# Graph attention with routed feed-forward: GpSimd's order in a block, the projection in two halves, and where the feed-forward tiles begin

## What is computed

```python
x = x + _L0_gnn_ref(_layernorm(x, axis=-1), adj, ...)
x = x + _L0_ffn_ref(_layernorm(x, axis=-1), ...)

# in _L0_gnn_ref: 4 heads of 32, the keys in 8 chunks of 128, a softmax in every chunk
scores = jnp.einsum('bhnd,bhjcd->bhnjc', q, kc) / jnp.sqrt(jnp.asarray(Dh, dtype=q.dtype))
scores = jnp.clip(scores, -10.0, 10.0)
scores = jnp.where(mask == 0, jnp.asarray(-10.0, scores.dtype), scores)
attn = jax.nn.softmax(scores, axis=-1)
ctx = jnp.einsum('bhnjc,bhjcd->bhnd', attn, vc)
out = ctx @ Wo.T + bo
out = out + x        # then a layer norm with gamma and beta

# in _L0_ffn_ref: 8 experts of 128 -> 256 -> 128, the two best of each row
gate_scores = x @ Wg + bg
_, idx = jax.lax.top_k(gate_scores, K)
h = jax.nn.gelu(jnp.einsum('td,edh->teh', xf, W1) + b1[None], approximate=False)
y = jnp.einsum('teh,ehd->ted', h, W2) + b2[None]
out = jnp.einsum('ted,te->td', y, mf)
```

## Time and profile before

| what | before |
|---|---|
| median of 3 runs | 852.67 us (850.55 to 852.83) |
| the profiled execution | 852.1 us, of which the span from first to last instruction is 850.5 |
| granted TensorE clock, mean | 0.96 |
| PE busy | 722.9 us (85% of the span) |
| DVE busy | 626.5 us (74%) |
| ACT busy | 491.2 us (58%) |
| POOL busy | 591.9 us (70%) |
| first clamp of scores | at 38.3 us |
| last clamp of scores | at 592.1 us |
| first tile turned | at 609.2 us |

### The profile page before, as it was taken

One profiled execution on the slowest core, in us unless ns is written; L12 is line 12 of the kernel. 1 busy time (PEld: TensorE's weight loads), 2 busy tenths in 40 slices (PEclk: granted clock), 3 DMA queues, 4 the chain that ended last, 5 costly groups with the idle time before them and its releaser, 6 DMA issues. The chain is left out here.

```text
span 850.5 us, 17280 instructions
## 1 busy us (share of the span) xinstructions
PE 722.9 (85%) x5499; PEld 377.7 (44%) x5499; DVE 626.5 (74%) x1472; ACT 491.2 (58%) x873; POOL 591.9 (70%) x674
## 2 busy tenths in 40 slices
PE   2688998998989989899899898787577879999994
PEld 1222233232333333333323333231277768999994
DVE  2178898898988989889898898989774544455552
ACT  2456666766667666676665765635244535666662
POOL 4697665978779787797886977848764556445553
PEclk9989999999999999999999999998787989999998
DMA  7100000011010110101100001003211246432330
GB/s 260 62 1 25 14 13 13 13 39 50 14 39 13 39 50 13 39 13 39 50 13 26 14 27 37 14 26 110 76 54 57 68 133 189 123 85 85 102 93 1
DMA packets 45255, 45.43 MB, mean 53 GB/s; under 512 B 7413, under 2 KB 39424, under 8 KB 44720
## 3 DMA queue, kind: packets, MB, share of 16 engines
q1 hardware_dynamic: 38800, 30.00, 12.6%
q0 software_dynamic: 6368, 14.34, 4.8%
HBM read 31.46 MB, written 18.34 MB: 59 GB/s over the span
## 5 line engine op out<-in xcount | busy, mean ns | idle before, releaser
L641 ACT ACTIVATE e<-e 128x2048 f32<-128x2048 f32 x128 | 244.3, 1910 | 184.1 <-DVE e L783 181.3
L783 DVE SCALAR_TENSOR_TENSOR e<-scores_ps,bound_mem 128x2048 f32<-128x2048 f32 x128 | 291.9, 2281 | 43.8 <-PE scores_ps L393 42.4
L1189 POOL DMA_INDIRECT out<-e,near x91 | 90.3, 993 | 100.2 <-DVE e L964 51.7
L1167 POOL TENSOR_TENSOR ctx_part<-ctx_part,z_inv 128x1024 f32<-128x1024 f32 x62 | 119.8, 1933 | 49.1 <-DVE z_inv L799 49.1
L706 ACT ACTIVATE e<-scores_ps,bound_mem 128x128 f32<-128x128 f32 x364 | 103.8, 368 | 71.0 <-PE scores_ps L532 55.5
L412 PE MATMUL z_ps<-e,one_column 128*32 128x512 f32 x1024 | 137.4, 609 | 0.0
L1179 POOL TENSOR_TENSOR ctx_sum<-ctx_sum,ctx_part 128x512 f32<-128x512 f32 x90 | 115.8, 1287 | 6.0
L532 PE MATMUL scores_ps<-e,bound_mem 128*128 128x128 f32 x728 | 103.3, 287 | 13.7 <-DVE bound_mem L946 7.6
L532 PEld LDWEIGHTS scores_ps<-e,bound_mem 128*128 128x128 f32 x728 | 93.6, 201 | 17.4 <-issue 11.0
L946 DVE COPY bound_mem<-bound_mem 128x258 f32 x182 | 51.3, 324 | 55.6 <-issue 54.9
L791 DVE STREAM_TRANSPOSE ctx_part<-ctx_ps 128x512 f32<-128x512 f32 x128 | 90.1, 704 | 0.1
(11 more groups left out here) (156 smaller groups left out, 1046.7 us busy)
## 6 DMA issues: line engine op xcount, KB each, us to landing
near<-sorted_rows SPq DMA_DIRECT2D x91, 130.0 KB
near<-in_x SPq DMA_DIRECT2D x16, 256.0 KB
bound_mem<-in_adjT SPq DMA_DIRECT2D x4, 1024.0 KB, 11.0
x_post<-in_x SPq DMA_DIRECT2D x16, 256.0 KB, 2.7
sorted_rows<-sorted_rows SPq DMA_DIRECT2D x16, 130.0 KB
sorted_rows<-sorted_rows POOLq DMA_DIRECT2D x12, 130.0 KB
out<-e,near POOLq DMA_INDIRECT x91
sorted_rows<-x_rows,slot POOLq DMA_INDIRECT x64
```

The source lines that it names most:

```text
L641: nc.scalar.activation(every, every, ACT.Exp, scale=SCORE_SCALE).then_inc(exp_done, 1)
L783: dve.scalar_tensor_tensor(out=e[:, s % E_RING], in0=scores_ps[:], scalar=-CLIP, in1=to, op0=ALU.max, op1=ALU.min).then_inc(clipped, 1)
L1167: nc.gpsimd.tensor_tensor(pair, pair, z_inv[:, v % 2, j:j + 2].to_broadcast([P, 2, SQUARES, DH]), ALU.mult).then_inc(ctx_scaled, 1)
L1189: nc.gpsimd.indirect_dma_start(out=out_rows, out_offset=bass.IndirectOffsetOnAxis(ap=near_u[:, id_at:id_at + 1], axis=0), in_=e_flat[:, at ...
```

## The change

**Attention.** On POOL the adding and scaling of contexts stands ahead of each root: `add_context` 1 and `scale` 2 come before the root of `ln2`, and `add_context` 3 and `scale` 4 before the residual, and so on. In block 15 the scatter of block 12 moves from behind all that to right behind the first `scale`. PE projects two of four row groups at j = 1 and two at j = 2 (block 13 all at once, as before); the input is now turned back into the bank by a transpose, and the context product is summed onto it. `rank` moves from j = 5 to j = 6. `normalise_x` moves from j = 7 to j = 0 of the next block.

**Feed-forward.** Block 16 is gone. Slot 0 holds the first tile's turn, then the context of step 126 and the gates of block 13, slot 1 the second tile's turn, the context of step 127 and the projection of block 14. DVE copies the first tile's weights ahead of turning the last contexts, and reads each tile's offsets one slot ahead. Everything else that hung on slots is written two or three slots later. The pads are 12 on SP (two behind each load from tile 28 on), 10 on POOL and 6 on ACT (both from slot 22 on).

```diff
-SP_PADS = 16
-PAD_LOAD, PAD_SLOT = 19, 21
+SP_PADS, POOL_PADS = range(0, 12), range(12, 22)
+ACT_PADS = range(22, NP)
+PAD_LOAD, PAD_SLOT = 28, 22
...
-                if i >= PAD_LOAD and n_padded < SP_PADS:
-                    pad(n_padded)
-                    n_padded += 1
+                for k in SP_PADS[max(2 * (i - PAD_LOAD), 0):max(2 * (i - PAD_LOAD) + 2, 0)]:
+                    pad(k)
...
-            def project(v):
+            def project(v, tiles=range(TILES)):
...
-                for t in range(TILES):
+                for t in tiles:
                     cols = slice(t * P, (t + 1) * P)
-                    pe.matmul(job_ps[1][:, cols], ctxT[:, cols], w_proj[:, W_O, :], start=True, stop=False)
-                    ins = pe.matmul(job_ps[1][:, cols], xnT_bo[:, v % 4, cols], ident[:], start=False, stop=True)
-                ins.then_inc(proj_filled, 1)
+                    pe.transpose(job_ps[1][:, cols], xnT_bo[:, v % 4, cols], ident[:])
+                    ins = pe.matmul(job_ps[1][:, cols], ctxT[:, cols], w_proj[:, W_O, :], start=False, stop=True,
+                                    skip_group_check=True)
+                if TILES - 1 in tiles:
+                    ins.then_inc(proj_filled, 1)
...
-            for u in range(FIRST, BLOCKS + 1):
-                for j in range(CHUNKS if u < BLOCKS else LAG):
+            for u in range(FIRST, BLOCKS):
+                for j in range(CHUNKS):
...
-                    if j == (2 if last else 1) and is_block(u - 2):
-                        project(u - 2)
+                    if last and j == 2:
+                        project(13)
+                    if not last and j in (1, 2) and is_block(u - 2):
+                        project(u - 2, range(2 * j - 2, 2 * j))
...
-                    if j == (1 if last else 5) and is_block(u - 3):
+                    if j == (1 if last else 6) and is_block(u - 3):
                         rank(u - 3)
...
             for k in range(SLOTS):
...
-                if k == 5:
+                if k == 8:
                     project(15)
...
                 if k < FFN_TILES:
                     turn_tile(k)
+                if k < LAG:
+                    context(STEPS - LAG + k)
+                if k == 0:
+                    gate(13)
+                if k == 1:
+                    project(14)
...
+            def pad(k):
+                at = act.value_load(pad_at[0:1, k:k + 1], min_val=0, max_val=SPARE * P)
+                act.dma_start(sorted_rows[bass.ds(at, P), :], sorted_tiles[SPARE]).then_inc(padded_act, 16)
...
+                    if j == 0 and is_block(u + 2):
+                        normalise_x(u + 2)
...
-                    if j == 7 and is_block(u + 3):
-                        normalise_x(u + 3)
...
+            load_offsets(0)
             for k in range(SLOTS):
+                if k < FFN_TILES:
+                    copy_weights(k)
+                if k + 1 < FFN_TILES:
+                    load_offsets(k + 1)
+                if k < LAG:
+                    turn(STEPS - LAG + k)
                 if k == 0:
-                    scale_last(4)
-                    scale_last(6)
...
+                    choose(13)
+                if k == 1:
+                    invert_sums(15)
+                if k == 2:
                     dve.wait_ge(proj_filled, 15)
                     statistics(ln["2"], 14, job_ps[1][:].rearrange("p (t d) -> p t d", d=D))
...
             for u in range(FIRST, BLOCKS):
+                last = u == BLOCKS - 1
                 if is_block(u - 1):
                     scale(u - 1, 0)
+                if last:
+                    scatter(u - 3)
...
```

161 lines of the change are left out of this document (85 added, 76 removed).

## The result

The changed kernel takes **814.93 us** (median of 4 runs, 813.95 to 816.87) beside 852.75 us of the kernel before on the same chip (4 runs): a ratio of 0.956, 95% interval 0.9529 to 0.9591. The forecast was 816.5 us, in a range of 805 to 831, with the chance on faster. The profiled execution took 816.87 us, with a span of 815.2.

A forecast was written before the change was run, and what follows sets the result against it. It took attention as held by DVE's 32.0 us of waits for POOL's sum, the ramp by waiting, steady tiles by PE. Gains 21.2 + 2.4 + 2.6 + 4.2 + 2.6 + 5.6 - 3.0 = 35.6 us: 852.1 to 816.5, range 805 to 831.

The forecast's parts named there:

- The contexts' sum: Attention: POOL's sum comes in time for DVE's turn, 1.5 of 2.03 us a block gained, 21.2 us in all.
- Rival B: Attention: another wait, root and normalise of `ln3`, takes the place of the wait for POOL's sum; 832 us, chance 0.08.
- The rank: Attention: moving `rank` to j = 6 frees the scores of step 6, 0.2 us in 12 blocks, 2.4 us gained.
- The half clock: Attention, start of blocks after 5, 8 and 12's boundaries: half a projection and less idle time save 2.6 us.
- The projection in halves: Attention, j = 1 and 2: half projections with transposes fit where PE waits; taken as zero, -0.5 to +0.4 us a block.
- Rival C: Attention: transposes and short pauses bring PE's half clock everywhere; 875 us at three stretches a block, chance 0.03.
- The ramp: From attention's last blocks to the steady tiles: waits shrink, 9.4 us gained in all.
- The first slots: Ramp, slots 0 to 9: slot 10 comes 1.5 us after old slot 7 with three tiles more done, 4.2 us gained.
- The early scatter: End of attention: block 12's scatter fills POOL's idle time; SP's first tile load goes sooner, inserted waits of 1.3 us covered.
- The middle: Ramp, the next 17 slots: loads no longer late once pads wait behind load 28, 2.6 us gained.
- ACT's pads: Ramp, slots 22 to 27: six pads on ACT, taken at SP's 1.5 us each, partly hidden, 3 us lost.
- SP's pace: Ramp, last 11 slots: SP's loads and pads no longer set the pace, slots fall to 1.90 us, 5.6 us gained.

The follow-up runs named there:

- e1: Kernel before with only POOL's new order in the attention blocks: 815.78 us against 842.04 us, ratio 0.9684.
- e2: Changed kernel with POOL's order in the blocks put back as before: 833.01 us against 842.04 us for the kernel before, ratio 0.9888.
- r1: Kernel before with POOL's new order and `rank` at step 6, ramp left old: 824.75 us against 852.75 us, ratio 0.9671.
- before_again: Kernel before, unchanged, run and traced again on a chip like that of the first record: 852.76 us.
- e3: Changed kernel with the projection whole at step 1, as two products per tile: 813.09 us against 842.04 us for the kernel before, ratio 0.9647.
- e5: Changed kernel with `normalise_x` back at the end of step 7: 808.52 us against 842.04 us for the kernel before, ratio 0.9595.
- e9: Changed kernel with block 15's projection one slot later in PE's queue: 816.43 us against 852.75 us for the kernel before, ratio 0.9571.
- e6: Changed kernel with block 12's scatter back at the end of POOL's last block: 817.81 us against 842.31 us for the kernel before, ratio 0.9712.
- e7: Changed kernel with no pads on ACT, 14 on SP and 14 on POOL: 816.57 us against 842.31 us for the kernel before, ratio 0.9686.

## Why the prediction was right, and where its terms were off

**Attention, foreseen 26.2 us, measured 25.25.** Its parts, by the blocks' lengths:
- *The contexts' sum, 21.2 us.* Right in mechanism and size. e1 takes a block from 34.80 to 33.33, 1.47 us where 1.5 was foreseen, since PE's scores are next late, as the prediction read from its rows of PE; block 2 gains 1.72. Twelve blocks and that one are 19.4 us, where 21.2 was foreseen. Rival B (another wait in its place) did not come.
- *The rank, 2.4 us.* Measured 0.21 us a block, 2.5 in all. What the prediction did not see is that it hangs on the first term: alone, with POOL late, it gives nothing (e2).
- *The half clock, 2.6 us.* In the trace of before three blocks were 0.99 us longer than the rest, 3.0 us, and all of it went. The reason given, half a projection and less idle time, is right in its second half: contexts in time are enough, with the whole projection (r1), and the halves with late contexts leave the half clock where it was (e2). The blocks named were chance: in before_again it was 11 and 14, and not 5, 8 and 12. The row of slices, which the prediction names for them, can't show them; the stretches of the trace do.
- *The projection in halves, zero.* Right (e3). Step 0 became 0.05 us longer (4.80 to 4.85), but with the contexts in time and not with the halves: e1 and r1 have it, e2 does not. The working behind the zero misread its row: the projection was eight products of 0.22 us, 2 us in all, and not sixteen; a half takes 0.9 us here and not up to 1.2. Rival C, a half clock from transposes, is refuted by the clock: transposes stand in two steps of every block's projection, and from 48 us to the last clamp the granted clock was 1.00. The Trainium skill (TensorE: Matmul & The Clock Gate, Part 4: PE-mode transpose) gives a transpose of 128x128 some 275 ns in a kernel, for bf16, and says that they don't keep the clock up. Here, in float32, four in a row took 0.65 us, 0.16 us each, and the clock stayed up with products between them.

**The ramp, foreseen 9.4 us, measured 9.5** in the first pair of traces and 13.7 in the second, of which 3.8 come from POOL's order alone; its own edits give 8.4 us by times (r1). On the chips of 842 us they give some 3 (e1, e5). The sum is right on the chip that it was made for, and that is luck in part, since its terms were off in both ways:
- *The first slots, 4.2 us.* This term was mis-sized. Foreseen was tile 10 at 1.5 us behind the old tile 7. Measured from the last clamp it is 47.8 - 43.8 = 4.0 us in the first trace, so 1.7 were gained, and 44.6 - 43.8 = 0.8 in the second, 4.9 gained. The step that added up DVE's list slot by slot missed that PE is queued behind DVE's turn of block 15's contexts in the same slot, 4.4 to 5.1 us. It also charged to DVE what is a chain over four engines: e9 takes the wait at the projection away and gets it back at the root.
- *The early scatter* stands in no term of its own, and is the largest: e6 loses some 10 us without it. It was treated under the end of attention as covered by the experts' loads; SP's 12.3 us wait had in fact set the start of everything in the slots.
- *The middle, 2.6 us, and ACT's pads, -3.0.* Together -0.4 was foreseen and 65.8 - 62.5 = 3.3 measured. The pads cost nothing (e7), since a pad holds ACT's queue for 0.53 us: the error was to take SP's price, with SP's idle times in it, for another engine. With them on ACT the last pad is in time for tile 37; without them, as e7 hangs them, 7.7 us are lost by ratio.
- *SP's pace, 5.6 us.* Measured 26.5 - 21.9 = 4.6: slots 33 and 34 took 2.08 and 2.55 us. On the chip of 842 us nothing of it is left: 11 slots took 26.7 us in e1 (24 to 34) and 28.2 in e5 (27 to 37), since PE comes to them sooner and SP does not.

Of the marks named in the prediction these came: blocks of 33.0 to 33.3 us, the last clamp in 565 to 568, DVE's wait gone but for a rest, SP's two waits gone, and less than 130 us to the steady pace. Only ACT late in slots 22 to 27 did not.

## What to carry to other kernels

Look for the in-order engine whose idle time stands ahead of the work that another engine will wait for, and fill it with work that needs nothing new: here that one reordering gives 26.3 us (e1) of the 33 to 38 of the whole change, while in attention the changes at the engine that was seen waiting (its products, its ranks) gave next to nothing without it (e2). In a section where the steps of a chain are written into slots by number, look first at what starts slot 0, and follow the chain over all engines before moving one of its steps: a wait that is removed at one turns up at the next. The price of moving a small DMA issue was that of the queue it was put on, and not of the one it was taken from: a pad held ACT's queue for 0.53 to 0.67 us where the prediction had taken 1.5 us from SP. And a gain in one section can be lost at the next bound: 10 us at tile 27 were nothing at tile 35 where SP's loads set the pace.
